# Decoder with two expert layers, one core: weighted rows added by accumulating scatters onto X + Y in memory

## What is computed

```
for e in range(E):
    we = jnp.sum(jnp.where(sel == e, rw, 0.0), axis=-1)
    h = jax.nn.silu(xf @ w1[e].T) * (xf @ w3[e].T)
    out = out + h @ w2[e].T * we[:, None]
```

## Time and profile before

| | |
|---|---|
| median of 3 runs | 2862.62 us (2862.38 to 2863.9) |
| the profiled execution, its own time | 2861.38 us |
| its span, first to last instruction | 2859.6 us |
| PE busy | 2420.2 us (85%) |
| DVE busy | 1628.9 us (57%) |
| ACT busy | 1130.6 us (40%) |
| POOL busy | 924.2 us (32%) |
| granted TensorE clock, mean | 0.896 |

### The profile page before, as it was taken

How to read it: one execution, slowest core, us unless ns; L and a number is a source line. 1 busy time by engine, 2 the same in 40 slices (tenths; PEclk the granted TensorE clock), 3 DMA queues, 4 the chain that set the end, 5 groups by cost and what they waited for, 6 DMA issues and landing times. The chain is left out here.

```text
span 2859.6 us, 44563 instructions
## 1 busy us (share of the span) xinstructions
PE 2420.2 (85%) x16004; PEld 1295.1 (45%) x16010; DVE 1628.9 (57%) x2579; ACT 1130.6 (40%) x2043; POOL 924.2 (32%) x740
## 2 busy tenths in 40 slices
PE   5678997866997995999999999777759999959996
PEld 4533335235886773333333332642622222248885
DVE  4778864654333334666666664246668999562223
ACT  2435664321000331444444444133426777712221
POOL 2521003311221112767767777122440000003331
PEclk8879998567998997999999999875869999969998
DMA  4432213425663555122222221442351111034555
GB/s 138 113 77 65 75 23 86 104 63 181 202 202 114 194 194 164 53 79 76 74 86 78 86 68 54 141 101 61 103 128 37 51 42 35 6 104 160 186 195 180
DMA packets 209626, 298.88 MB, mean 105 GB/s; under 512 B 51289, under 2 KB 149619, under 8 KB 208950
## 3 DMA queue, kind: packets, MB, share of 16 engines
q1 hardware_dynamic: 182326, 227.86, 25.9%
q0 software_dynamic: 22944, 63.99, 7.7%
q10 hardware_dynamic: 4192, 4.85, 0.9%
HBM read 205.03 MB, written 90.92 MB: 103 GB/s over the span
## 5 line engine op out<-in xcount | busy, mean ns | idle before, releaser
L1609 ACT ACTIVATE a_probs<-a_cols 128x512 f32<-128x512 f32 (+3 forms) x896 | 445.2, 549 | 242.8 <-PE a_cols L1539 162.9
L1631 DVE TENSOR_REDUCE a_mxw<-a_rows 128x2 f32<-128x1024 f32 (+1 forms) x448 | 475.7, 1100 | 66.7 <-PE a_rows L1497 41.6
L2058 DVE TENSOR_REDUCE a_mxw<-a_rows 128x2 f32<-128x1024 f32 x256 | 313.4, 1224 | 209.8 <-PE a_rows L1896 208.0
L2036 ACT ACTIVATE a_probs<-a_cols 128x1024 f32<-128x1024 f32 x256 | 261.7, 1024 | 268.9 <-PE a_cols L1925 253.6
L1877 POOL TENSOR_TENSOR a_sums<-a_sums,a_probs 128x1024 f32<-128x1024 f32 x128 | 309.3, 2416 | 105.7 <-ACT a_probs L2036 92.7
L1539 PE MATMUL a_cols<-a_qs,a_ks 50*128 50x512 bf16 (+7 forms) x1792 | 275.1, 363 | 14.9 <-DMA a_qs<-a_nparts 8.8
L2315 PE MATMUL e_psU<-e_xT,e_w 128*128 128x256 f32 x1216 | 271.4, 381 | 1.9 <-ACT e_xT L2362 1.2
L1921 PE MATMUL a_cols<-a_qf,a_kf 64*128 64x512 f32 x1024 | 267.9, 601 | 0.1
L1567 PE MATMUL a_out<-a_probs,a_vs 128*17 128x256 f32 (+4 forms) x3328 | 256.0, 381 | 0.2 <-ACT a_probs L1609 0.2
L1497 PE MATMUL a_rows<-a_ks,a_qs 48*128 48x512 bf16 (+3 forms) x896 | 174.7, 386 | 90.6 <-DVE a_mxw L1631 43.7
L1939 PE MATMUL a_out<-a_probs,a_vs 128*64 128x512 f32 x1024 | 248.6, 606 | 0.0
(11 more groups left out here) (274 smaller groups left out, 3295.6 us busy)
## 6 DMA issues: line engine op xcount, KB each, us to landing
e_w<-in_w SPq DMA_DIRECT2D x69, 512.0 KB
e_w<-in_w SPq DMA_DIRECT2D x30, 1024.0 KB
a_qs<-q_scratch SPq DMA_DIRECT2D x336, 64.0 KB, 2.3
qk_wide_scratch<-t_f SPq DMA_DIRECT2D x32, 512.0 KB, 2.9
q_scratch<-t_parts POOLq DMA_DIRECT2D x56, 192.0 KB, 2.6
a_ks<-k_scratch SPq DMA_DIRECT2D x144, 64.0 KB, 2.4
vw_scratch<-t_v SPq DMA_DIRECT2D x8, 1040.0 KB, 4.6
a_vs<-vw_scratch SPq DMA_DIRECT2D x16, 520.0 KB, 6.7
```

Source lines behind the costliest of these rows:

```text
L1609: act.activation(pr[ug % RING][:, 2 * hp + e, c0:512], psC[(2 * at + e) % 3][:, 0:512 - c0], ACT.Exp, scale=scale).then_inc(ex_done, 1)
L1631: dve.tensor_reduce(mxw[w][:, a, hp, :, t % 4:t % 4 + 1], src[:, :, 0:n], AX.X, ALU.max).then_inc(s_free, 1)
L2036: act.activation(pr[i][:], psC[i % 2][:], ACT.Exp, scale=scale).then_inc(ex_done, 1)
L2058: dve.tensor_reduce(mxw[:, j % 2, :, j // 2:j // 2 + 1], psR[:], AX.X, ALU.max).then_inc(s_free, 1)
```

## The change

The results of the experts no longer go to places of their own in memory to be loaded, weighted and added at the stage's end. Instead:

- In t2 and t6, SP stores each chunk of X to a new array in memory, after the chunk's `y_free` (L714's signal), in t2 to `sums_scratch`, in t6 to the output itself; the first chunk also into 256 spare rows behind the T rows. The output array is therefore T + 256 rows long, and the host leaves the last 256 out.
- At the start of e2 and e6, POOL adds all of Y onto that array with one accumulating DMA of 2 MB, ahead of the gathers.
- ACT stores the table of weights (K * T floats) to memory, DVE computes two more index lists (`onto`, the row a slot adds to; `weight_at`, its place in the table), and for each piece POOL gathers the weights of 2 x 128 slots by two more indirect DMAs of 4 bytes per partition, into `of_slot`.
- DVE takes each tile of `psD` by itself, multiplies it by the slot's weight (in e2 after adding the bias) and signals; POOL scatters each tile as soon as it is ready, with accumulation onto the array. Because two pieces may add to the same row, the scatters of piece j wait until those of piece j-1 have landed (`stored`), those of piece 0 until Y has been added.
- `psD` has one buffer per tile, not per piece. PE waits for each tile's `y_ready` by itself.
- L2483 (X + Y), L2238, L2492 and L2244 are gone. In e2 SP loads the finished sums back to X in eight chunks, each with a semaphore on which t3's chunk waits; e6 ends with the last scatter.
- The prefetch of t3's weights moves from the start of SP's work in e2 to behind the weights of piece 2.

```
@@ token_stage
                     elif wide is not None:
                         store_sets(sp, back)
                         store_values(sp, back)
+                    elif sums is not None:
+                        c, p, r = back
+                        sp.wait_ge(y_free, c + 1)
+                        for first in (c * C, T)[:1 + (c == 0)]:
+                            sp.dma_start(sums[first:first + C, :].rearrange("(t p) d -> p t d", p=P),
+                                         G["X"][:, c * CT:(c + 1) * CT, :]).then_inc(x_stored, 16)
                 in_halves(step)
+                if sums is not None:
+                    sp.wait_ge(x_stored, 16 * (NC + 1))
...
+                    if rows_loaded is not None:
+                        dve.wait_ge(rows_loaded[c], 16)
                     moments(lambda t: row_of(c, t), norm == "rms")
@@ moe_stage, SP
-                if prefetch:
-                    prefetch.load(sp)
+                    if prefetch and isinstance(j, int) and j == 2:
+                        prefetch.load(sp)
...
                 for p in range(2):
                     sp.wait_ge(stored[p], 16 * RT * uses[p])
-                for q in range(4):
-                    for k in range(K):
-                        at = (k * NT + q * QUARTER) * P
-                        sp.dma_start(got[:, k, q * QUARTER:(q + 1) * QUARTER, :],
-                                     results[at:at + QUARTER * P, :].rearrange("(t p) d -> p t d", p=P)
-                                     ).then_inc(fetched[q], 16)
-                if out is not None:
...
+                if reload is not None:
+                    for c in range(NC):
+                        sp.dma_start(G["X"][:, c * CT:(c + 1) * CT, :],
+                                     sums[c * C:(c + 1) * C, :].rearrange("(t p) d -> p t d", p=P)).then_inc(reload[c], 16)
@@ moe_stage, POOL
+                def gather_weights(j):
+                    p = j % 2
+                    for t in range(RT):
+                        n = j * RT + t
+                        pool.indirect_dma_start(of_slot[p][:, t:t + 1], None, table_of_weights[0:P * KN, :],
+                                                bass.IndirectOffsetOnAxis(ap=weight_at[:, n:n + 1], axis=0)
+                                                ).then_inc(w_ld[p], 16)
                 def scatter(j):
                     p = j % 2
-                    pool.wait_ge(y_ready, j + 1)
+                    if j:
+                        pool.wait_ge(stored[1 - p], 16 * RT * ((j - 1) // 2 + 1))
+                    else:
+                        pool.wait_ge(y_added, 16)
                     for t in range(RT):
+                        pool.wait_ge(y_ready, RT * j + t + 1)
                         n = j * RT + t
-                        pool.indirect_dma_start(results, bass.IndirectOffsetOnAxis(ap=to[:, n:n + 1], axis=0),
-                                                yo[p][:, t, :], None).then_inc(stored[p], 16)
+                        pool.indirect_dma_start(sums, bass.IndirectOffsetOnAxis(ap=onto[:, n:n + 1], axis=0),
+                                                yo[p][:, t, :], None, compute_op=ALU.add).then_inc(stored[p], 16)
+                pool.dma_start(sums[0:T, :].rearrange("(t p) d -> p t d", p=P), G["Y"][:], accum_op=ALU.add).then_inc(y_added, 16)
                 pool.wait_ge(indices_ready, 1)
                 gather(0)
                 gather(1)
+                pool.wait_ge(slot_weights_ready, 1)
+                pool.wait_ge(table_stored, 16)
+                gather_weights(0)
+                gather_weights(1)
                 for j in range(NJ):
                     if j + 2 < NJ:
                         gather(j + 2)
                     scatter(j)
+                    if j + 2 < NJ:
+                        gather_weights(j + 2)
@@ moe_stage, PE
-                        wait(pe, y_ready, j - 1)
                         for t in range(RT):
+                            wait(pe, y_ready, RT * (j - 1) + t + 1)
...
-                                mm = pe.matmul(psD[p][:, t, :], h[p][:, m, t * P:(t + 1) * P], w2s[p][:, m, :],
+                                mm = pe.matmul(psD[t][:], h[p][:, m, t * P:(t + 1) * P], w2s[p][:, m, :],
                                                start=(m == 0), stop=(m == NF - 1))
-                        mm.then_inc(d_ready, 1)
+                            mm.then_inc(d_ready, 1)
@@ moe_stage, ACT
+                act.wait_ge(weight_ready, 1)
+                act.dma_start(table_of_weights[0:P * KN, :].rearrange("(p s) a -> p (s a)", p=P),
+                              weight[:].rearrange("p k t -> p (k t)")).then_inc(table_stored, 16)
@@ moe_stage, DVE
+                dve.tensor_scalar(row_of[:], to[:], P - 1, KN.bit_length() - 1, ALU.bitwise_and, ALU.logical_shift_left)
+                dve.tensor_scalar(column_of[:], to[:], P.bit_length() - 1, KN - 1, ALU.logical_shift_right, ALU.bitwise_and)
+                dve.tensor_scalar(beyond[:], to[:], K * T, K - 1, ALU.bitwise_and, ALU.logical_shift_right)
+                dve.drain()
+                dve.tensor_tensor(weight_at[:], row_of[:], column_of[:], ALU.add)
+                op(dve.tensor_tensor(onto[:], fro[:], beyond[:], ALU.add))
+                signal(slot_weights_ready)
...
-                    dve.wait_ge(d_ready, j + 1)
                     wait(dve, stored[p], 16 * RT * r)
-                    if affine:
-                        dve.tensor_tensor(yo[p][:], psD[p][:], b2s[p][:], ALU.add).then_inc(y_ready, 1)
-                    else:
-                        dve.tensor_copy(yo[p][:], psD[p][:]).then_inc(y_ready, 1)
-                    if isinstance(j, int) and j < 2:
-                        for q in (2 * j, 2 * j + 1):
-                            some = slice(q * QUARTER, (q + 1) * QUARTER)
-                            dve.tensor_tensor(X[:, some, :], X[:, some, :], G["Y"][:, some, :], ALU.add)
+                    dve.wait_ge(w_ld[p], 16 * RT * (r + 1))
+                    for t in range(RT):
+                        dve.wait_ge(d_ready, RT * j + t + 1)
+                        rows_of_t = psD[t][:]
+                        if affine:
+                            dve.tensor_tensor(biased[:, t, :], psD[t][:], b2s[p][:, t, :], ALU.add)
+                            dve.drain()
+                            rows_of_t = biased[:, t, :]
+                        dve.tensor_scalar(yo[p][:, t, :], rows_of_t, of_slot[p][:, t:t + 1], None, ALU.mult).then_inc(y_ready, 1)
                 two_halves_odd(dve, NJ, step)
-                dve.drain()
-                for q in range(4):
-                    dve.wait_ge(fetched[q], 16 * K)
-                    for k in range(K):
-                        for t in range(q * QUARTER, (q + 1) * QUARTER):
-                            ins = dve.scalar_tensor_tensor(X[:, t, :], got[:, k, t, :], weight[:, k, t:t + 1],
-                                                           X[:, t, :], ALU.mult, ALU.add)
...
```

62 lines of the change are left out of this document (32 added, 30 removed).

## The result

The kernel after takes 2835.89 us, the median of four runs (2831.68 to 2838.47), where the kernel before took 2862.5 (2854.58 to 2863.9): a ratio of 0.9914, 95% interval 0.9899 to 0.9928, so 20.6 to 28.9 us less. The profiled execution took 2831.68 us with a span of 2829.8. The direction and the range held; the time is 5.9 us above the forecast of 2830.

The account below looks back on a forecast made before the run. PE bounds the pieces, so expert stages lose time only at their starts and ends. Terms -24.0 - 6.9 - 0.9 - 1.0 + 0.5 = -32.3 us from the median 2862.6 gave 2830 us, range 2822 to 2846.

Parts of the forecast that it names:

- End of e6: Kernel's end: result loads, additions and stores of X go, one scaling and scatter landing stay; -24.0 us (-25.0 to -19.2).
- End of e2: End of e2: tile scatter lands, then SP's eight loads end the stage and t3 starts earlier; -6.9 us (-8 to -3).
- X + Y out of the pieces: Pieces of e2 and e6: up products no longer slowed by DVE adding X and Y; -0.9 us (-1.1 to 0).
- Start of e2: Start of e2: prefetch leaves, but Y's adding stands ahead of the gathers in POOL's queue; -1.0 us (-5 to +5).
- Start of e6: Start of e6: Y's adding hidden up to about 25 us, new index lists and weights' gathers cost nothing; 0.
- Stores of X: t2 and t6: stores stand before later chunk loads in SP's order, so delays may show; +0.5 us (0 to +3).
- Inside the pieces: Pieces of e2 and e6: POOL's extra transfers, the `stored` wait and the moved prefetch stay covered; 0 (0 to +3).
- through by 725: e2: prefetch and weights of pieces 2 and 3 finish by 725 at 362 GB/s, 5 us before piece 3 starts.
- the gathers behind Y: Rival, 0.14: in POOL's queue gathers cannot pass Y, which is slow beside the weights; e2's start +5, total 2838 to 2846.
- The end of e2 gives nothing: Rival, 0.10: SP's eight load issues take 0.91 us each and block, or t3 waits for chunks; 2836 to 2838.
- the new wait binds: Rival, 0.06: in e6's pieces an adding scatter lands after more than 9.5 us; at 10 us +11, 2841.
- Adding in memory is slow: Rival, 0.06: Y's transfer ahead of the gathers takes over 39 us, making the kernel slower; at 50 us, 2885.

Follow-up runs that it names:

- before_moved: The kernel before with only t3's prefetch moved from ahead of the pieces to behind piece 2's weights: 2863.57 us, ratio 1.0013.
- before_hold: before_moved, with SP also waiting for piece 0's gathers before issuing piece 1's weights: 2858.39 us.
- no_y: prefetch_last without the transfer adding Y in memory and its wait, so the output lacks Y: 2837.11 us.
- after_again: The kernel after, unchanged, run and profiled once more: 2831.98 us, ratio 0.9893 to the kernel before.
- prefetch_first: The kernel after with t3's prefetch back at the head of SP's work in e2, as in the kernel before: 2844.04 us, ratio 0.9935.
- prefetch_last: The kernel after with t3's prefetch issued behind all pieces of e2 instead of behind piece 2's weights: 2834.19 us, ratio 0.9913.

## Why the prediction came out as it did, by its own steps

*End of e6: -24.0 forecast, -19.9 measured*, inside its ends and near the worse one. The chain behind PE's last product, forecast and then measured: scaling 0.49 and 0.52; start of the last scatter 0.27 and 0.99; landing 3.41 (2.41 and 1.0 for the adding) and 3.7; behind the landing nothing and 3.1. The estimate for the adding was good. Two steps failed. "Its scatter is issued by then" had three terms wrong. Tile 0's issue was taken at 0.97 us; it takes 1.55. It was given a start 0.27 us behind its `e_y`; it began 0.77 behind it, though POOL had stood idle for 7.36 us, and why is not shown. And tile 0 was said to be ready 2.2 us before tile 1; the earlier trace rows show there the turn of a next piece (0.44), which the last piece doesn't have, and the two `e_y` are 1.63 apart. Together 0.77 + 1.55 + 0.30 - 1.63 = 0.99. The other step is that the sum ended with the landing: POOL's DRAIN (1.7 us) and the closing of the stage (1.4) come behind it. That 3.1 us is the larger part of the miss. The closing is in the kernel before too (2858.3 to 2859.6); the DRAIN was there as well, but hidden, and came to the end only with the change. Both were left out because the timeline of instructions doesn't list what the sequencers do.

*End of e2: -6.9 and -6.5.* Landing 3.7 instead of 3.4, the eight loads 4.2 instead of 4.1. The split into tiles paid for the extra work, as the sum had it.

*X + Y out of the pieces: -0.9 and some -0.5.* The up products of pieces 1 and 2 are at 7.07 in e2 (713.85 above). In e6 the difference is below what two profiles of one kernel differ by. The 0.5 is counted in the 3.7 that e2's pieces grew by. (Four times 0.26 would be 1.0, not the 0.9 of the forecast.)

*Start of e2: -1.0 and -0.4.* The number is near and its reason was wrong. "Without the prefetch up to 4.9 us are to be had" is refuted by before_moved (1.1) and before_hold (5.0, once piece 1's weights are held too): of the 8.2 us of the earlier trace rows 1.1 belong to the prefetch and 3.5 to piece 1's weights. In the kernel after the gather was quick all the same, and the loads became late, the second bias last, since Y's adding takes DMA time and SP's issues take longer beside it (without Y the start is 1.7 us shorter: no_y). That two opposite moves came out near -1.0 is luck.

*Start of e6: 0 and -0.3. Stores of X: +0.5 and +0.4* (t2 unchanged, t6 49.0 to 49.4; t6 has 48.8 to 49.7 in the three profiles without these stores, so the 0.4 can't be told from nothing).

*Inside the pieces: 0 (0 to +3) and +4.1.* The new wait for `stored` never bound: in e6 the slowest scatter landed 7.4 us after its start (the view of `e_onto` from 2580 on), and the next piece's comes 8.9 us behind it, so 1.5 us were left. The pieces without the stall last 14.25 us in e2 as before. What failed is the cover of the prefetch, "through by 725". The transfers were to run at 362 GB/s, but from 700 to 710, where the prefetch is issued and POOL's gathers and scatters run between, they did 212 and 292 (238 and 259 in after_again), and the weights were through by 728.5; by estimate, 8.2 MB from 701 on are 298 GB/s. The forecast also left out SP's issues and the loads of the biases: with b1's issue hanging for 7.41 us, the last load came 1.8 us behind the weights. And the price of a wait had no term for the clock, which made 4.1 us of 2.3; the fall to 0.67 behind a wait of PE was in the earlier trace rows to be seen.

So the sum should have been -23.5 rather than -32.3: 4.1 us at the last end, 4.1 in the piece, 0.6 at the start of e2. From the median of 2862.6 that gives 2839.1, still inside the stated range. The measured median came nearer to the forecast, 2835.9 against 2830, and that is luck: its four runs lie 6.8 us apart, and those of the kernel before 9.3.

Of the rivals, *the gathers behind Y* had the mechanism right and the condition not met. In the kernel after, Y landed at 658.6 + 16.1 = 674.7, one us after the gather's issue (673.64), and the gather lost nothing by it: 5.4 us, where it takes 6.3 without Y (no_y, 681.86 to 688.11). In prefetch_first Y landed at 691.4 and the gather right behind it. The rule of the Trainium skill that stood beside this rival (DMA: Bandwidth & Descriptors, "Queues, rings and completion order") agrees with both. The seven idle us that were put against the rival decided: SP's weights were issued from 668.4 on, when Y had run for 9.8 us. *The end of e2 gives nothing* and *the new wait binds* did not come. *Adding in memory is slow*: Y landed 16.1 us after its issue in e2, far from 39; a plain load of its size took 7.4. The 16 us are mostly its own: in e6, where SP issues the first weights at 2555.7 only, it took 16.0, and before them the window reads

```profile
2550.00:2555.00 5.00, 0.61 (x2) 0.13 (x2) 3.65 (x16) 0.22 (x1) 0.00 (x0) 0.50 1.23 193
```

## To carry to other kernels

Cut the end of a stage at every step up to the barrier, the closing of each queue included: the last landing of a software transfer is not the end of the stage, and what used to hide POOL's drain may be the very work that the change removes. Before moving a load, ask which load nobody needs yet is already in the way: in the kernel before, holding one piece's weights back gave 4.0 us, moving 3.6 MB of prefetch 1.1. Ask too whether a wait names more loads than its reader needs: both waits of PE in the kernel after ended with a bias that the up products don't read; a wait of its own for that bias was not tried. And a stall of PE is to be priced with the clock behind it, 4.1 us for 2.3 of waiting here.

## What the runs showed of the hardware that was not expected

- An adding scatter of 128 rows of 1 KB holds POOL for 1.58 us against 0.99 for one that overwrites, and lands after 3.7 rather than 2.4 us at best, 5.9 rather than 2.8 at the median.
- POOL's DRAIN at the end of a stage ends 1.4 to 1.7 us after its last scatter has landed when nothing or one load of 256 KB is moving, and 3.5 to 6.1 us after it beside SP's four to eight loads.
- A transfer of 2.1 MB that adds in memory took 16.0 to 16.1 us with other loads beside it in its second half only, and 29.2 beside the prefetch and the weights; a gather behind it in POOL's queue could be used 1.0 us after it had landed.
- The DMA engines can be full (share 1.23) at 193 GB/s while a 2 MB transfer in rows of 1 KB is added in memory and nothing else is loaded; with plain weights and prefetch a share of 1.01 to 1.06 carries 357 to 422 (before_moved and before_hold, 715 to 730).
- A DVE instruction of two on-chip operands and 0.16 us takes 0.90 beside an addition on POOL.
- An issue on SP's queue that takes 0.44 us took 7.41 behind 3.6 MB of prefetch and 2.1 MB of weights that were under way, and 9.17 behind the prefetch and the weights in prefetch_first.
- A wait of PE of 1.13 us ahead of a piece left the granted clock at 1.00, one of 1.94 us was followed by 8.86 us for products of 7.07.
